# Writing out the loops of a layered attention kernel, with semaphores that only count up

## The reference

```python
x = x + layernorm(attention(layernorm(x)))        # 16 heads of 16, rotary, full softmax over 2048 keys
x = x + layernorm(local_transformer(layernorm(x)))
# local_transformer: 2 layers, each
#   h = shift_token(x); q, k, v = split(h @ wqkv)      8 heads of 64
#   q, k = rotary_xpos(l2norm(q) * qs, l2norm(k) * ks)
#   x = x + local_attention(q, k, v, window=128) @ wo   each block of 128 looks at itself and the one before
#   h = layernorm(shift_token(x)) * lg + lb; a, g = split(h @ w1 + b1)   hidden size 682
#   x = x + (a * gelu(g)) @ w2 + b2
```

## Time and profile before

| what | value |
|---|---|
| median of 3 runs | 3102.14 us (3088.32 to 3109.27) |
| profiled execution, its own time | 3115.37 us |
| its span, first to last instruction | 3113.4 us |
| mean granted TensorE clock | 0.947 |
| projection stage, up to about | 180 us |
| attention stage | 180 to 1680 us |
| output stage | 1680 to 1760 us |
| feed-forward half | 1760 to 3113 us |

### The profile page before, as it was taken

How to read it: one execution, slowest core, us unless ns; L and a number is a source line. 1 busy time by engine, 2 the same in 40 slices (tenths; PEclk the granted TensorE clock), 3 DMA queues, 4 the chain that set the end, 5 groups by cost and what they waited for, 6 DMA issues and landing times. The chain is left out here.

```text
span 3113.4 us, 63400 instructions
## 1 busy us (share of the span) xinstructions
PE 2918.7 (94%) x23360; PEld 1798.8 (58%) x23360; DVE 2424.1 (78%) x4390; ACT 2266.6 (73%) x4928; POOL 1136.8 (37%) x1617
## 2 busy tenths in 40 slices
PE   8969999999999999999998689999999899999996
PEld 5733333333333333333334478888888788888885
DVE  4668988989889897988972577777777777878774
ACT  3506877878778786877877667777777777787774
POOL 3610000000000000000002666666666667777774
PEclk9967998999999998989999899999999999999998
DMA  3332333233323332433223100000001200000000
GB/s 107 128 85 38 61 60 62 45 61 65 57 51 55 65 57 41 65 57 59 47 44 136 54 5 4 3 3 3 3 3 45 75 8 16 17 17 17 17 17 28
DMA packets 74411, 138.77 MB, mean 45 GB/s; under 512 B 21760, under 2 KB 43712, under 8 KB 67520
## 3 DMA queue, kind: packets, MB, share of 16 engines
q1 hardware_dynamic: 69696, 134.88, 20.6%
q10 hardware_dynamic: 4544, 1.38, 0.2%
HBM read 88.63 MB, written 43.38 MB: 42 GB/s over the span
## 5 line engine op out<-in xcount | busy, mean ns | idle before, releaser
L700 DVE TENSOR_REDUCE mx<-aux 128x1 f32<-128x1024 f32 x1024 | 1247.8, 1224 | 164.3 <-PE aux L565 157.1
L670 ACT ACTIVATE probs<-scores 128x512 f32<-128x512 f32 x2048 | 1118.5, 596 | 303.5 <-PE scores L589 202.2
L565 PE MATMUL aux<-k_stack,q_stack 48*128 48x512 f32 x2048 | 815.4, 478 | 31.4 <-DMA k_stack<-qk_dram 22.7
L589 PE MATMUL scores<-q_stack,k_stack 50*128 50x512 f32 x2048 | 803.2, 469 | 13.3 <-ACT probs L670 13.3
L601 PE MATMUL pv<-probs,v_ones 128*32 128x256 f32 x8192 | 692.8, 412 | 0.1
L589 PEld LDWEIGHTS scores<-q_stack,k_stack 50*128 50x128 f32 x2048 | 327.3, 194 | 459.4 <-ACT probs L670 437.7
L533 POOL CAST w_raw_hi<-w_raw 128x576 fp32r<-128x576 f32 x30 | 20.1, 670 | 1216.5 <-DMA w_raw<-in_ff_weights 1216.5
L601 PEld LDWEIGHTS pv<-probs,v_ones 128*32 128x32 f32 x8192 | 165.0, 110 | 387.1 <-ACT probs L670 256.4
L565 PEld LDWEIGHTS aux<-k_stack,q_stack 48*128 48x128 f32 x2048 | 330.1, 199 | 84.5 <-DVE mx L700 52.8
L1428 ACT ACTIVATE probs<-probs,negmax 128x256 f32<-128x256 f32 (+1 forms) x512 | 249.9, 490 | 88.1 <-DVE negmax L1511 88.1
L1220 POOL TENSOR_TENSOR rnorm<-norm_min,minus_half 128x8 f32<-128x8 f32 x128 | 234.8, 1835 | 10.7
(11 more groups left out here) (184 smaller groups left out, 5589.6 us busy)
## 6 DMA issues: line engine op xcount, KB each, us to landing
q_stack<-qk_dram SPq DMA_DIRECT2D x192, 128.0 KB, 4.8
k_stack<-qk_dram SPq DMA_DIRECT2D x192, 128.0 KB, 6.5
w_raw<-in_ff_weights SPq DMA_DIRECT2D x30, 288.0 KB, 9.3
split_dram<-w_raw_hi SPq DMA_DIRECT2D x30, 288.0 KB, 2.1
split_dram<-w_raw_lo SPq DMA_DIRECT2D x30, 288.0 KB, 2.3
qk_dram<-qkT_hi SPq DMA_DIRECT2D x32, 256.0 KB, 3.1
qk_dram<-qkT_lo SPq DMA_DIRECT2D x32, 256.0 KB, 3.6
x_ring<-x_dram SPq DMA_DIRECT2D x32, 128.0 KB, 3.5
```

Of the source, the lines that this page charges most:

```text
L565: last = nc.tensor.matmul(aux[:, ring["unit"], block_of_keys % 2], q_stack[rows, r % BODY, tile * P:(tile + 1) * P], k_stack[rows, r % BOD ...
L589: nc.tensor.matmul(scores[:, item % BANKS1], k_stack[0:SCORE_ROWS, r % BODY, s * P:(s + 1) * P], q_stack[0:SCORE_ROWS, r % BODY, j * 512:( ...
L670: nc.scalar.activation(probs[:, item % PROBS], scores[:, item % BANKS1], ACT.Exp, scale=float(D1) ** -0.5).then_inc(probs_ready, 1)
L700: nc.vector.reduce_max(mx[:, slot, tile, half:half + 1], aux[:, unit].rearrange("p a k -> p (a k)"), AX.X).then_inc(max_taken, 1)
```

## The change

The streams of TensorE, ScalarE and VectorE in the attention stage, and of all engines in the output stage and the feed-forward half, are written out step by step. Every wait is for the running count since the stage began, and there are no decrements. `Waiter`, `walk` and the segments go; `Step` loses its turn and skipped count. SyncE and GpSimd keep their loop over heads, with its decrements, in the attention stage (`looped_heads`). What an instruction computes, which engine does it and in what order stays. The small semaphores within VectorE's and GpSimd's own chains (`maxima_written`, `rsum_made`, `pool_step`) still count down.

```diff
-UNROLL = 4
-
-
 class Step:
 
 
-    def __init__(self, t, skipped, turn, tiles):
-        self.t, self.skipped, self.turn = t, skipped, turn
-        self.tiles = tiles
+    def __init__(self, t, tiles):
+        self.t, self.tiles = t, tiles
 
     def exists(self, d):
-        return 0 <= self.t + self.skipped + d < self.tiles
+        return 0 <= self.t + d < self.tiles
 
     def layer(self, d):
-        return (self.t + self.skipped + d) // NT
+        return (self.t + d) // NT
 
     def first(self, d):
 
...
-class Waiter:
-
-
-
-    def __init__(self, eng):
-        self.eng, self.sems, self.fallen = eng, {}, {}
-
-    def on(self, sem, per_step, when=lambda step: True):
-
-        self.sems[sem.name] = (sem, per_step, when)
-        self.fallen[sem.name] = 0
-        return sem
-
-    def upto(self, sem, count):
-
-        self.eng.wait_ge(sem, count - self.fallen[sem.name])
-
-    def fall(self, steps):
-        for sem, per_step, when in self.sems.values():
-            rises = per_step * sum(when(step) for step in steps)
-            if rises:
-                self.eng.sem_inc(sem, -rises)
-                self.fallen[sem.name] += rises
-
-
-def walk(waiter, segments, tiles):
-
-    t, skipped = segments[0][0], 0
-    for first, steps, turns in segments:
-        assert first == t + skipped
-        if turns:
-            with waiter.eng.Fori(0, turns) as turn:
-                body = [Step(t + i, skipped, turn, tiles) for i in range(steps)]
-                yield from body
-                waiter.fall(body)
-                t += steps
-            skipped += (turns - 1) * steps
-        else:
-            for _ in range(steps):
-                yield Step(t, skipped, None, tiles)
-                t += 1
+def steps_of(first, last, tiles):
+
+    return [Step(t, tiles) for t in range(first, last + 1)]
 
...
-        DVE_ITEMS = len(aux_items(2)) - 1
 
         def first_unit(left):
             return len(aux_items(1)) % UNITS if left == 0 else 0
 
-        def body_of_heads(eng, head, m, per_head, per_slot):
-
-            for r in range(BODY):
-                head(r, m * BODY + r, 2)
-            for semaphore, rises in per_head:
-                eng.sem_inc(semaphore, -BODY * rises)
-            for semaphores, rises in per_slot:
-                for semaphore in semaphores:
-                    eng.sem_inc(semaphore, -rises)
-
-        def all_heads(eng, head, per_head, per_slot=(), looped=True):
-
-            if looped:
-                with eng.Fori(0, (NH - 2) // BODY) as m:
-                    body_of_heads(eng, head, m, per_head, per_slot)
-            else:
-                for m in range((NH - 2) // BODY):
-                    body_of_heads(eng, head, m, per_head, per_slot)
+        def looped_heads(eng, head, per_head):
+
+            with eng.Fori(0, (NH - 2) // BODY) as m:
+                for r in range(BODY):
+                    head(r, m * BODY + r, 2)
+                for semaphore, rises in per_head:
+                    eng.sem_inc(semaphore, -BODY * rises)
             head(0, NH - 2, 1)
             head(1, NH - 1, 0)
+
+        def written_out_heads(head):
+
+            for n in range(NH):
+                head(n, min(NH - 1 - n, 2))
...
-            def head(r, n, left):
-                if r == 0:
-                    ring.update(start, last=list(start["last"]))
+            def head(n, left):
                 for d, s in steps():
-                    step(r, d, s, left)
+                    step(n, d, s, left)
 
...
-            start = dict(ring, last=list(ring["last"]))
-            all_heads(pe, head, ((m_parts_made, 1), (v_made, 1), (pv_copied, 1), (probs_ready, BLOCKS * TB), (max_taken, DVE_ITEMS), (rows_freed, 1)),
-                      ((for_max_loaded, 16 * LOADS), (for_scores_loaded, 16 * LOADS), (rows_loaded, 16)), looped=False)
+            written_out_heads(head)
...
-            all_heads(act, head, ((rows_in_psum, 1), (scores_ready, BLOCKS * TB), (pv_done, TB)))
+            written_out_heads(head)
...
-                if r == 0:
-                    taken[0] = start
...
-            start = taken[0]
-            all_heads(dve, head, ((max_in_psum, DVE_ITEMS),))
-
...
-OUT_SEGMENTS = ((-2, 7, 0), (5, UNROLL, 6), (29, 8, 0))
...
+OUT_STEPS = steps_of(-2, NT + 4, NT)
...
-SEGMENTS = ((-3, 6, 0), (3, UNROLL, 6), (27, 10, 0), (37, UNROLL, 6), (61, 8, 0))
+STEPS = steps_of(-3, LAYERS * NT + 4, LAYERS * NT)
...
-            w = Waiter(dve)
-            w.on(for_dve, 1, lambda step: sum(r == "dve" and here(step, d, of_pair) for _, d, r, _, of_pair in ITEMS))
-            for s_, n in ((squares_made, 2), (sin_rnorm_made, 4), (gate_made, 3), (hrstd_made, 1), (x_b2_made, 1), (hstats_made, 1),
-                          (cos_made, 1), (rot_made, 1), (exps_made, 4), (rsums_made, 2), (xT_rounded, 1), (oT_rounded, 1)):
-                w.on(s_, n)
-            w.on(hT_rounded, NC, of_second), w.on(up_arrived, 32, lambda step: step.exists(0))
-            w.on(fstats_made, 1, last_layer(-4)), w.on(frstd_made, 1, last_layer(-5))
-            w.on(cos_table_made, 1, lambda step: step.exists(2) and step.tile_of_pair(2) == 0)
...
-            for st in walk(w, SEGMENTS, LAYERS * NT):
+            for st in STEPS:
...
-                    w.upto(xT_rounded, t + 3)
+                    dve.wait_ge(xT_rounded, t + 3)
```

More of the change, by code:

```diff
@@ L670, in exponentiate, with head @@
                 nc.scalar.activation(probs[:, item % PROBS], scores[:, item % BANKS1], ACT.Exp, scale=float(D1) ** -0.5).then_inc(probs_ready, 1)
-            def head(r, n, left):
+            def head(r, left):
                 for d, s in steps():
@@ L938, in nth_last @@
 def nth_last(step, d):
-    before = sum((turns - 1) * steps for first, steps, turns in SEGMENTS if turns and first < NT)
-    return step.t + before + d - (LAYERS - 1) * NT
+    return step.t + d - (LAYERS - 1) * NT
 def starts_layer(step, d):
-    at = step.t + step.skipped + d
-    return at // NT if step.turn is None and at in (0, NT) else None
+    return (step.t + d) // NT if step.t + d in (0, NT) else None
 def item_counts():
     ready, freed, n = {}, {}, {"ready": {"act": 0, "dve": 0}, "freed": {"act": 0, "dve": 0, "pool": 0}}
-    t, skipped = SEGMENTS[0][0], 0
-    for first, steps, turns in SEGMENTS:
-        for _ in range(steps):
-            step = Step(t, skipped, None, LAYERS * NT)
-            for name, d, reader, _, of_pair in ITEMS:
-                if here(step, d, of_pair):
-                    n["ready"][reader] += 1
-                    ready[name, t + d] = n["ready"][reader]
-            for reader, names in FREES.items():
-                for name, d, of_pair in names:
-                    if here(step, d, of_pair):
-                        n["freed"][reader] += 1
-                        freed[name, t + d] = n["freed"][reader]
-            t += 1
-        skipped += (turns - 1) * steps if turns else 0
+    for step in STEPS:
+        for name, d, reader, _, of_pair in ITEMS:
+            if here(step, d, of_pair):
+                n["ready"][reader] += 1
+                ready[name, step.t + d] = n["ready"][reader]
+        for reader, names in FREES.items():
+            for name, d, of_pair in names:
+                if here(step, d, of_pair):
+                    n["freed"][reader] += 1
+                    freed[name, step.t + d] = n["freed"][reader]
     return ready, freed
@@ L1132, in _ @@
         def _(sp):
-            w = Waiter(sp)
-            w.on(x_summed, 1, last_layer(-5)), w.on(x_mid_made, 1, lambda step: step.exists(1))
             sp.wait_ge(zero_made, 2)
-            for st in walk(w, SEGMENTS, LAYERS * NT):
-                at = None if st.turn is not None else st.t + st.skipped
-                if at == NT - 3:
+            for st in STEPS:
+                if st.t == NT - 3:
                     for i in range(2):
@@ L1246, in _ @@
         def _(pe):
-            w = Waiter(pe)
-            w.on(by_act, len(FREES["act"])), w.on(by_pool, 3)
-            w.on(by_dve, 1, lambda step: sum(here(step, d, of_pair) for _, d, of_pair in FREES["dve"]))
-            w.on(x_staged, 1), w.on(rotary_done, 1)
             last_in_bank = {}
@@ L1407, in _ @@
         def _(act):
-            w = Waiter(act)
-            w.on(for_act, 1, lambda step: sum(r == "act" and here(step, d, of_pair) for _, d, r, _, of_pair in ITEMS)), w.on(max_made, 4)
-            w.on(fnmr_made, 1, last_layer(-5))
             act.wait_ge(loaded_act, 48)
@@ L1417, in item @@
             def item(name, v):
-                w.upto(for_act, ready[name, v])
+                act.wait_ge(for_act, ready[name, v])
                 return bank(name)
-            for st in walk(w, SEGMENTS, LAYERS * NT):
+            for st in STEPS:
                 t = st.t
@@ L1536, in _ @@
             drained = 0
-            for st in walk(w, SEGMENTS, LAYERS * NT):
+            for st in STEPS:
                 t = st.t
```

(4 more changed lines are left out.)

176 lines of the change are left out of this document (79 added, 97 removed).

## The result

The changed kernel takes 2999.4 us (median of 4 runs, 2990.8 to 3013.6) against 3095.2 us before (3073.3 to 3109.3): a ratio of 0.970, 95% interval 0.963 to 0.977. On another chip it was 0.971 (0.961 to 0.980). The profiled execution has a span of 2992.9 us, 120.5 less than before.

A forecast was written before the change was run, and what follows sets the result against it. TensorE, busy 94% of the span and partly at the low clock, was taken as the bound. Savings of 78 + 17.1 + 5.3 = 100 us from 3115.4 gave 3015, or 3002 by the median; forecast 3010, range 2990 to 3045.

The forecast's parts named there:

- (a): Attention: without TensorE's decrements, ten heads lose pauses (13.3 us) and low-clock stretches (65 us), 78 us saved, bounds 13 and 80.
- (b): Attention: removing the branches and decrements of ScalarE and VectorE gains nothing further, being covered by TensorE's pause; 0 us.
- (c): Feed-forward half: ends of passes vanish, 9.0 us in the first loop and 8.1 in the second, 17.1 us saved.
- (d): Output stage: six ends of a pass at 0.88 us each vanish, 5.3 us saved.
- (e): Stage borders, projection stage, layer change and last steps stay as before; 0 us.
- the clock that falls anyway: Rival, attention: a limit on dense stretches lowers the clock regardless, so only pauses go; 3080 or 3066 us; chance 0.06.
- some falls remain: Rival, attention: other TensorE pauses still bring four low-clock stretches of 6.5 us each; 3041 us; chance 0.05.
- Slow instruction supply: Rival, attention: written-out ScalarE or VectorE runs dry, pausing TensorE; 3249 us if once in each of 30 heads; chance 0.03.

The follow-up runs named there:

- d15_every_head: The changed kernel with 15 additions to an unused semaphore in TensorE's attention stream after each of the first 30 heads; one execution, 3169.0 us.
- f15_feed_forward_pause: The changed kernel with 15 semaphore additions in TensorE's feed-forward stream after every fourth step of the former loops, twelve times; one execution, 3002.7 us.

## Why the prediction was right

The forecast was 3010 and the measured median 2999, by the steps that were given.

(a) The heads. 78 us were expected, of them 13.3 pause and 65 clock; the ten heads gave 78.3. That figure was read from the same execution that it is now compared with, so it was bound to fit once no fall was left. That the pause is TensorE's 15 decrements and not ScalarE's or VectorE's loop is shown by the two kernels that have the one without the other. That the pause makes the clock fall is shown too, with a correction: it makes it likely. The kernel before had a fall after each of its ten in the trace that I read; the two other kernels with these decrements had seven and eight of ten, and pauses in every head about one in two. In their executions the term is 66 and 64. The 78 is one draw of something that varies, and that the medians agree with it is partly luck.

(b) Nothing for ScalarE's and VectorE's streams: right, 1302.0 against 1303.3 us.

(c) The feed-forward half: 17.1 expected, 19.6 measured. The sum was right for the first loop (484.01 to 476.58 us is 7.4). In the second loop the reference was mis-sized: the first pass, 79.79, was taken as undisturbed, and undisturbed is 79.38, so six passes gave 9.1 us without the last way out. That leaves 3.1 us for the two ways out. "Addresses through registers cost nothing" holds for the first loop alone. The kernel with decrements and without loops has 79.40 at this place, so the 0.4 us are not the decrements but come with the looped code; whether with its registers wasn't separated.

(d) The output stage: 5.3 expected, 5.4 measured.

(e) Nothing for the other stages: right for the change. The profiled executions differ by 17 us there, by the time of the clock's first rise and the first head's low clock. The 13 us between the profiled execution and the median of before were put down to the low-clock stretches of attention or to profiling; the start of the program is a third source that I had not seen, and of the same size. In the profiled pair it fell to the side of the change, so the 120.5 us between the two executions are not a measure of it.

Of the rivals, the clock that falls anyway is excluded by 1338 us at the full clock in the changed kernel, and by the falls that followed 25 of 30 pauses of 1.3 us in the three traces with TensorE's decrements. That some falls remain holds in a small way: one in eight traces, in place of the four in each that the rival priced. Slow instruction supply didn't appear: the instruction queues moved 3.85 MB in place of 2.50, and no new pause stands in any stream.

## What to carry to other kernels

Look for a pause of TensorE just ahead of each low-clock stretch, even a pause of a microsecond, and price the pause with the slow stretch behind it: here 13 us of pauses cost 64 to 78, themselves included. Bookkeeping on TensorE's own queue (a decrement took it 0.15 us here, and fifteen of them idled it for 1.3 us at each end of a pass in attention) belongs in no dense stretch like this one; semaphores that count on need none of it, and that edit alone, on one engine, gives some three quarters (78 of the 103 us that the traces put down to the change) of what writing out all streams gives. Test a gain of the clock with more than one execution, since it varies: ten such pauses were followed by ten falls in one trace, by seven and by eight in two others.

## What the runs showed of the hardware that I had not expected

- In attention, pauses of TensorE of 1.30 to 1.40 us: 25 falls in thirty, and 16 in thirty where every head had one. Of 0.85 to 1.02 us: no fall at the ten that were put in, and one fall at the two that came by themselves (0.97 us; none at 0.85).
- After a pause of 1.3 us the low clock lasted 3.4 to 47.8 us in attention, and in the feed-forward half 3.4 to 6.8 us after one of 2.6. In attention TensorE was busy throughout, for 47.00 of 47.00 us in the longest (765 to 812 us of d15_every_head). The longest stretch that the changed kernel has left lies around the start of attention: PEclk 0.50 from 154 to 246 us.
- The first rise after the start came at 20 to 61 us from execution to execution, worth up to 19 us (the projection stage ended between 151.4 and 170.0), and keeping TensorE busy from the start didn't make it early: 57.7 and 28.7 us in the two traces.
- The same 15 semaphore additions idled TensorE for 1.3 us in attention (d15_every_head), and for 0.34 us in the feed-forward half (f15_feed_forward_pause), where they cost 0.46.
